# Routed third feed-forward: the second half's token rows scattered one per tile over sixteen tiles instead of two per tile over eight

## Chip, cores, metric

One core of one Trainium2 chip runs the whole program. The metric is device time in microseconds (us) of one execution. "Faster" or "slower" below is always against the kernel before.

## What is computed

Four layers, each an attention-like block and a feed-forward block, over x of 4 batches x 512 tokens x 128 features, f32. The change touches the third feed-forward, a mixture of 8 experts of which each token takes two:

```python
logits = jnp.einsum('bsd,de->bse', x, Wg)
top_vals, top_idx = jax.lax.top_k(logits, 2)
weights = softmax(top_vals) put at top_idx
for e in range(8):
    u, v = x @ W1[e], x @ W2[e]            # 128 -> 256 each
    out += ((u * sigmoid(u) * v) @ W3[e]) * weights[..., e][..., None]
```

## The kernel before, in words

Each engine has its own instruction stream; they meet at semaphores. The kernel doesn't run all experts over all tokens. It sorts the (token, choice) rows by expert into tiles of 128 rows, so that each tile belongs to one expert, and runs one small matrix chain per tile. The 4 batches are done in two halves (batches 0 and 1, batches 2 and 3). A half has HT = 8 token tiles and K1 = 2 choices, so 16 scatters of 128 rows each, and TILES2 = 23 expert tiles; NTILE2 = 46 tiles run in one unrolled loop over c. Tiles 0 to 22 are the first half, 23 to 45 the second.

What each engine does around the change:

- POOL (GpSimd). `scatter_in(half, i)` (L812) is an indirect DMA that writes 128 rows of 129 numbers (a token row and its row number) from SBUF into the table `tiles_in` in HBM, to the places that the routing found; each adds 16 to the semaphore `scattered`. `scatter_out(c)` (L831) waits for tile c's result (`y2_ready`) and writes its 128 rows with an indirect DMA into the table `tiles_out`. POOL runs its stream strictly in order. The first half's 16 scatters in are done before the loop. In the loop (L836 to L840) POOL does `scatter_out(c)`, and behind it, for c = 3 to 10, two of the second half's scatters in. I call the second half's scatters in by number, in 0 to in 15, and the scatters out by tile, out 0 to out 45.
- SP (SyncE) issues the loads of `tiles_in` in pairs of tiles (L690). Tiles sit in groups: 0-7, 8-15, 16-22, 23-30, 31-38, 39-45. The loads of group n wait until all scatters out of group n-2 have landed (L688). Before the first load of the second half (tile 23) SP also waits until all 16 of the second half's scatters in have landed (L706). Behind the loads of group 4 (tiles 31 to 38) it issues the loads of the first half's results (L700), which wait for out 22.
- PE (TensorE), in iteration c: `turn_in2(c+1)` (L1661) transposes the next tile and waits for its load; `up2(c)`; `turn_hidden2(c-1)` (L1684); `down2(c-2)`; then `beside_tiles(c)`. One of these calls is `load_word(1, w)` at c = 10, 13, 16: PE reads a word of SBUF into a register that says which experts the second half's tiles belong to. It is first used at c = 23 and waits for DVE's step `tiles2_1` (L3060).
- DVE (VectorE), in iteration c: `product2(c)` (L3126), `copy_hidden2(c-1)` (L3133), `copy_y2(c-2)` (L3141), which writes the result y of tile c-2. `copy_y2` of group 2 and later waits until the scatters out of group n-2 have landed, since the buffer is reused. At c = 28, 29 `combine2` (L3152, L3157) weighs the first half's two choices.
- ACT (ScalarE), in iteration c: `copy_in2(c+1)` and `gate2(c)`, both L1884, both waiting for PE.

So y of tile c comes in iteration c+2, behind the transposition of tile c+3, and everything on PE behind a transposition that waits for its load waits too. L853 is the helper for all other matmuls.

Of the kernel before, what the change touches and what calls it, by code (L numbers as in the profile page):

```python
# [35 lines left out]
E1, F1, K1 = 16, 176, 2  # L36
# [10 lines left out]
HT = 2 * TT  # L47
# [53 lines left out]
def build(nc, a, out):  # L101

    with ExitStack() as ctx:
# [6 lines left out]
        def sem(name):  # L110
            if name not in held:
                held[name] = ctx.enter_context(nc.semaphore(name))
            return held[name]
# [132 lines left out]
        def rows_of_choice(b, k):  # L246

            return token_rows[K1 * b + k]
# [484 lines left out]
        def _(pool):  # L733
# [72 lines left out]
            def scatter_in(half, i):  # L806

                t, k = divmod(i, K1)
                b = HALVES[half][t // TT]
                pool.wait_ge(setup, SETUP.index(f"places2_{half}") + 1)  # L810
                pool.wait_ge(sem("h_rows_ready"), NB + b + 1)
                nc.gpsimd.indirect_dma_start(  # L812
                    out=tiles_in, out_offset=bass.IndirectOffsetOnAxis(ap=routes2[half].scatter_at[:, k * HT + t:k * HT + t + 1], axis=0),
                    in_=rows_of_choice(b, k)[:, t % TT, :], in_offset=None, bounds_check=NTILE2 * P - 1,
                    oob_is_err=False).then_inc(sem("scattered"), 16)
# [11 lines left out]
            def scatter_out(c):  # L827
                group, slot = y2_place(c)
                pool.wait_ge(*tile_loaded(c))
                pool.wait_ge(sem("y2_ready"), c + 1)  # L830
                nc.gpsimd.indirect_dma_start(  # L831
                    out=tiles_out, out_offset=bass.IndirectOffsetOnAxis(ap=x2_in[:, slot, D:D + 1].bitcast(U32), axis=0),
                    in_=y2_rows[:, slot, :], in_offset=None, bounds_check=K1 * NTOK - 1,
                    oob_is_err=False).then_inc(y_stored[group % 2], 16)

            for c in range(NTILE2):  # L836
                scatter_out(c)
                if 3 <= c < 3 + HT:
                    for k in range(K1):
                        scatter_in(1, K1 * (c - 3) + k)  # L840

            for b in range(NB):
                pool.wait_ge(sem("rows3_ready"), b + 1)
# [4 lines left out]
        def _(pe):  # L848
# [752 lines left out]
            def count2(half, at):  # L1601

                chosen = routes2[half].chosen
                pe.wait_ge(setup, SETUP.index(f"chosen2_{half}") + 1)
                mm(psum[:, at, 0:HT * E2], before[:], chosen, True, False, skip_group_check=True)
                for t in range(1, HT + 1):
                    m = mm(psum[:, at, t * E2:(HT + 1) * E2], ones_b[:], chosen[:, 0:(HT + 1 - t) * E2], False, t == HT, skip_group_check=True)
                m.then_inc(sem("counted1"), 1)
# [17 lines left out]
            def load_word(half, w):  # L1626
                if w == 0:
                    pe.wait_ge(setup, SETUP.index(f"tiles2_{half}") + 1)
                words[half, w] = nc.tensor.value_load(routes2[half].tile_words[0:1, w:w + 1], min_val=0, max_val=8 ** 8 - 1)
# [77 lines left out]
            def turn_back2(b, at):  # L1707

                pe.wait_ge(sem("combined"), NB + b + 1)
                for t in range(TT):  # L1710
                    m = nc.tensor.transpose(psum[:, at, t * P:(t + 1) * P], gathered2[:, b % 2 * TT + t, 0, :], eye[:])
                m.then_inc(sem("batch_out"), 1)

            def center3(b, at):
                pe.wait_ge(x_ready, x_after(FFN2, b))
                mm(bank(at), center[:], x[:, b, :]).then_inc(sem("ln_centered"), 1)

            def variance3(b, at):
                pe.wait_ge(sem("ln_squared"), norm_of(ATTN3, b))
                pe.wait_ge(sem("ln_copied"), b + 1)  # L1720
                mm(bank(at), mean[:], squares3[b % 2]).then_inc(sem("ln_var"), 1)

            def project3(b, at):
                pe.wait_ge(ln_done, norm_of(ATTN3, b))
                mm(bank(at), w_3[:, W_IN, :], h[:, b, :]).then_inc(sem("proj3_done"), 1)

            def gate_x3(b, at):
                pe.wait_ge(sem("xw_ready"), b + 1)
                mm(bank(at), w_3[:, W_GX, :], xw[b % 2]).then_inc(sem("proj3_done"), 1)

            def gate_a3(b, at):

                if at >= 6:
                    pe.wait_ge(sem("gx_ready"), b + 1)
                mm(bank(at), w_3[:, W_GA, :], xw[b % 2]).then_inc(sem("proj3_done"), 1)
# [41 lines left out]
            def beside_tiles(c):  # L1777
                n = c - TILES2
                if c == 1:
                    pe.wait_ge(setup, SETUP.index("scores2_1") + 1)  # L1780
                    pe.wait_ge(sem("h_rows_ready"), NB + 3)
                    count2(1, 7)
                if c in (10, 13, 16):
                    load_word(1, (c - 10) // 3)
                for b in range(2):
                    at = 6 + b
                    if n == 6 + b:
                        turn_back2(b, at)
                    if n == 8 + b:
                        center3(b, at)  # L1790
                    if n == 10 + b:
                        variance3(b, at)
                    if n == 14 + b:
                        project3(b, at)
                    if n == 16 + b:
                        gate_x3(b, at)
                    if n == 18 + b:
                        gate_a3(b, at)

            turn_in2(0)  # L1800
            for c in range(NTILE2 + 2):
                if c + 1 < NTILE2:
                    turn_in2(c + 1)
                if c < NTILE2:
                    blocks[c] = block_of(c)
                    up2(c)
                if 1 <= c < NTILE2 + 1:
                    turn_hidden2(c - 1)
                if c >= 2:
                    down2(c - 2)  # L1810
                beside_tiles(c)
# [67 lines left out]
        def _(act):  # L1879
# [199 lines left out]
            def shared_gates(b):  # L2079
                act.wait_ge(sem("shared_up"), 2 * b + 2)  # L2080
                if b >= 1:

                    act.wait_ge(sem("shared_hid"), b)
                lo, _, hi = ((0, 4, 5), (2, 3, 1))[b % 2]
                f(shared_act0, bank(lo), ACT.Silu).then_inc(sem("shared_gate"), 1)
                f(shared_act1[HI:HI + F1R], psum[0:F1R, hi, :], ACT.Silu).then_inc(sem("shared_gate"), 1)
# [305 lines left out]
        def _(dve):  # L2392
# [408 lines left out]
            for _, hi in shared_hid:  # L2801
                v.memset(hi, 0.0)
# [4 lines left out]
            def shared_products(b):  # L2807
                _, up, hi = ((0, 4, 5), (2, 3, 1))[b % 2]
                for n, (src, gates_, dst, rr) in enumerate(((up, shared_act0, shared_hid[b % 2][0], slice(0, P)),
                                                            (hi, shared_act1, shared_hid[b % 2][1], slice(HI, HI + F1R)))):  # L2810

                    dve.wait_ge(sem("shared_gate"), 2 * b + n + 1)
                    dve.wait_ge(sem("shared_up"), 2 * b + 2)
                    if b >= 2:
                        dve.wait_ge(sem("shared_out"), b - 1)
                    m = v.tensor_tensor(dst[rr], psum[rr, src, :], gates_[rr], ALU.mult)
                m.then_inc(sem("shared_hid"), 1)
# [467 lines left out]
```

## Time and profile before

| | |
|---|---|
| median of 3 runs | 1105.28 us (1103.7 to 1110.93) |
| the profiled execution | 1108.78 us, its span 1107.0 us |
| busy share of the span | PE 84%, DVE 54%, ACT 45%, POOL 27% |
| tile loop of the third feed-forward | first matmul at about 885 us, last scatter out at 1016.79 us |
| granted TensorE clock over the span | 0.92 of full |

Times in the rows are us from the span's start. A timeline row is: start, duration, engine, line, operation, output<-input, count, and in brackets how long the engine had been idle and what ended that. Rows with a count merge neighbours. "issue" is a wait that nothing in the profile explains, "remote" one that ended with a semaphore event which the profile can't give to an engine of this core. PE's ends are modelled, not measured.

### The profile page before, as it was taken

The numbers are of one execution on the slowest core, as the hardware profiler recorded it, in microseconds if no ns is written. First come the engines' busy times: TensorE is split into PE (matmuls) and PEld (weight loads), VectorE is DVE, ScalarE is ACT, GpSimd is POOL, SyncE is SP. The second block draws the span as 40 slices with busy tenths as digits, with TensorE's granted clock in tenths as the row PEclk, the third lists the DMA queues.
The fourth block names the chain that finished last, engine by engine and source line by source line (L and its number), as shares of the span: only waits on it lengthen the run. The fifth ranks groups of instructions, "written<-read, shape, count | busy, mean of one in ns | idle before, by whom it ended". The sixth has DMA issues, their size and how long they took to land.

```text
span 1107.0 us, 12051 instructions
## 1 busy us (share of the span) xinstructions
PE 931.5 (84%) x3714; PEld 425.8 (38%) x3714; DVE 601.3 (54%) x1207; ACT 499.6 (45%) x937; POOL 300.9 (27%) x303
## 2 busy tenths in 40 slices
PE   5799999999799999998767984957877776887788
PEld 2344545454222222332233761422332344554433
DVE  2223233433888878777224445379998542545355
ACT  4233223233267667777632331665755421445720
POOL 9100000000001110110363561056756645433010
PEclk9799999999899999999969996988988886988889
DMA  8660000040011211210232206000000201311023
GB/s 175 183 235 0 1 1 1 1 93 0 23 52 49 77 49 51 59 43 3 55 105 70 56 26 189 8 11 1 0 1 7 69 28 53 100 33 50 3 77 114
DMA packets 81329, 59.52 MB, mean 54 GB/s; under 512 B 23422, under 2 KB 75704, under 8 KB 81172
## 3 DMA queue, kind: packets, MB, share of 16 engines
q1 hardware_dynamic: 74932, 51.00, 16.8%
q0 software_dynamic: 6336, 7.77, 2.3%
q8 instruction: 31, 0.51, 0.2%
q14 instruction: 30, 0.25, 0.1%
HBM read 38.41 MB, written 21.87 MB: 54 GB/s over the span
## 4 chain that ended last, share of the span: by engine, by line
PE 62%; DVE 12%; issue 11%; ACT 7%; another core or an unknown queue 2%; POOL 2%; SPq 2%; DMA 2%; DVEq 0%; POOLq 0%; ACTq 0%
PE psum L853 59%; ACT sb_scr L1884 3%; DVE sb_scr L2604 3%; DVE sb_scr L2979 2%; DVE sb_scr L2988 2%; POOL sb_scr L800 1%; ACT sb_qstack L1884 1%; ACT psum L1884 1%; SPq L629 1%; PE psum L1684 1%; PE psum L1009 1%; PE psum L1661 1%; SPq L634 0%; DVE sb_scr L2466 0%
## 5 line engine op out<-in xcount | busy, mean ns | idle before, releaser
L1884 ACT ACTIVATE sb_scr<-psum 128x512 f32<-128x512 f32 (+5 forms) x592 | 298.6, 539 | 367.1 <-PE psum L853 243.2
L2604 DVE TENSOR_REDUCE sb_scr<-psum 128x2 f32<-128x1024 f32 x128 | 154.7, 1222 | 40.3 <-PE psum L853 40.0
L761 POOL DMA_DIRECT2D sb_heads<-sb_scr x48 | 24.8, 523 | 439.6 <-DVE sb_scr L2620 439.3
L853 PE MATMUL psum<-sb_wide,sb_scr 128*128 (+1 forms) x532 | 120.8, 356 | 7.0 <-DVE sb_scr L3141 5.5
L800 POOL TENSOR_TENSOR sb_scr<-sb_scr 128x512 f32<-128x512 f32 x64 | 82.7, 1298 | 99.0 <-ACT sb_scr L1884 53.1
L853 PE MATMUL psum<-sb_kstack,sb_qstack 96*128 96x512 bf16 x256 | 98.2, 395 | 8.2 <-DVE sb_scr L2604 8.1
L853 PE MATMUL psum<-sb_qstack,sb_kstack 128*128 128x512 bf16 x256 | 99.0, 393 | 4.2 <-ACT sb_scr L1884 2.8
L2530 DVE TENSOR_SCALAR sb_scr<-psum,sb_b 128x512 f32<-128x512 f32 x48 | 34.6, 748 | 116.4 <-PE psum L853 116.4
L1884 ACT ACTIVATE sb_scr<-psum,sb_b 128x512 f32<-128x512 f32 x48 | 31.3, 685 | 142.9 <-PE psum L853 142.9
L853 PE MATMUL psum<-sb_h,sb_wide 128*128 128x512 f32 x192 | 88.3, 596 | 0.8 <-ACT sb_scr L1884 0.8
L853 PEld LDWEIGHTS psum<-sb_wide,sb_scr 128*128 128x128 f32 x532 | 76.4, 202 | 30.4 <-issue 28.5
L2979 DVE TENSOR_TENSOR_SCAN sb_scr<-psum,sb_scr 128x512 f32<-128x512 f32 x64 | 77.9, 1217 | 13.8 <-ACT psum L1884 13.7
L853 PE MATMUL psum<-sb_scr,sb_v 128*32 128x512 f32 x512 | 70.8, 625 | 4.8 <-ACT sb_scr L1884 4.2
L853 PE MATMUL psum<-sb_wparts,sb_pick 96*128 96x512 bf16 x128 | 43.0, 419 | 36.8 <-DVE sb_scr L2988 36.1
L853 PE MATMUL psum<-sb_scr,sb_eye 128*128 128x512 f32 x128 | 73.3, 658 | 0.8 <-DVE sb_scr L2988 0.5
L831 POOL DMA_INDIRECT tiles_out<-sb_scr x46 | 44.9, 976 | 74.2 <-DVE sb_scr L3141 62.5
L853 PEld LDWEIGHTS psum<-sb_qstack,sb_kstack 128*128 128x128 bf16 x256 | 24.9, 98 | 97.3 <-ACT sb_scr L1884 75.3
L853 PE MATMUL psum<-sb_scr,sb_wide 128*128 128x512 f32 x128 | 60.4, 594 | 0.0
L3126 DVE TENSOR_TENSOR sb_scr<-psum,sb_scr 128x256 f32<-128x256 f32 x46 | 19.5, 425 | 56.1 <-ACT sb_scr L1884 47.6
L789 POOL DMA_INDIRECT expert_out<-sb_scr,sb_row_at x40 | 38.9, 972 | 37.2 <-DVE sb_row_at L2839 15.0
L853 PEld LDWEIGHTS psum<-sb_h,sb_wide 128*128 128x128 f32 x192 | 34.5, 193 | 33.0 <-issue 31.9
L853 PE MATMUL psum<-sb_x,sb_center 128*128 128x512 f32 x64 | 37.8, 685 | 7.9 <-DVE sb_x L2624 5.2
(338 smaller groups left out, 1367.0 us busy)
## 6 DMA issues: line engine op xcount, KB each, us to landing
sb_qstack<-q_bounce SPq DMA_DIRECT2D x48, 96.0 KB
sb_kstack<-k_bounce SPq DMA_DIRECT2D x144, 32.0 KB
sb_scr<-pick_rows SPq DMA_DIRECT2D x8, 512.0 KB
sb_scr<-tiles_in SPq DMA_DIRECT2D x22, 129.0 KB
expert_in<-sb_scr SPq DMA_DIRECT2D x4, 645.0 KB, 6.1
tiles_in<-sb_scr SPq DMA_DIRECT2D x4, 645.0 KB, 8.3
sb_scr<-expert_in SPq DMA_DIRECT2D x8, 322.5 KB, 3.5
expert_out<-sb_scr SPq DMA_DIRECT2D x4, 512.0 KB, 4.9
```

Of the source, the lines that this page charges most:

```text
L629: sp.dma_start(weights1[q][0][:, :, at:at + hi - lo], a[f"L1_ffn_w_{n}"][2 * q:2 * q + 2, :, lo:hi].rearrange("e d f -> d e f")).then_inc( ...
L761: pool.dma_start(heads[at:at + DH, b % 2, :], head_out(n)[32 * j:32 * j + DH, :]).then_inc(sem(f"heads_packed{b % 2}"), 16)
L789: nc.gpsimd.indirect_dma_start(out=expert_out, out_offset=bass.IndirectOffsetOnAxis(ap=row_at[:, q % RX, j:j + 1], axis=0), in_=y_rows[:, ...
L800: nc.gpsimd.tensor_tensor(drive[:, n % RB, :], dtx[:, b, :], bcast_b[:, n % RB, :], ALU.mult).then_inc(sem("drive_ready"), 1)
L831: nc.gpsimd.indirect_dma_start(out=tiles_out, out_offset=bass.IndirectOffsetOnAxis(ap=x2_in[:, slot, D:D + 1].bitcast(U32), axis=0), in_=y ...
L853: return nc.tensor.matmul(out_, w, r, start=start, stop=stop, **kw)
L1884: return nc.scalar.activation(out_, in_, func, **kw)
L2530: v.tensor_scalar(hidden[:, c % 2, t, :], bank(t), b1[:, t, c:c + 1], 0.0, ALU.add, ALU.max).then_inc(sem("hid_dve"), 1)
L2604: v.reduce_max(headmax[:, g % 2, t:t + 2, j], banks, AX.X).then_inc(sem("maxed"), 1)
L2979: v.tensor_tensor_scan(state[:, i % RB, :], bank(4 + i % RD), drive[:, i % RB, :], 0.0, ALU.mult, ALU.add).then_inc(sem("scanned"), 1)
L2988: v.tensor_tensor(read[:, i % 2, :], bank(2 + i % RC), state[:, i % RB, :], ALU.mult).then_inc(sem("read_ready"), 1)
L3126: v.tensor_tensor(hid2[:, c % 2, :], psum[:, UP2_BANKS[c % 3], H2:2 * H2], gact2[:, c % 2, :], ALU.mult).then_inc(sem("hid2_ready"), 1)
```

## The change

POOL: behind each scatter out of tiles 3 to 18 there is one scatter in instead of two behind each of tiles 3 to 10. PE: the three `load_word(1, w)` are at c = 5, 6, 7 instead of 10, 13, 16. Nothing else differs.

```diff
             for c in range(NTILE2):
                 scatter_out(c)
-                if 3 <= c < 3 + HT:
-                    for k in range(K1):
-                        scatter_in(1, K1 * (c - 3) + k)
+                if 3 <= c < 3 + K1 * HT:
+                    scatter_in(1, c - 3)
@@ PE, beside_tiles(c)
-                if c in (10, 13, 16):
-                    load_word(1, (c - 10) // 3)
+                if c in (5, 6, 7):
+                    load_word(1, c - 5)
```

## Rows read from the trace of the kernel before

**Rows 1.** The page: the chain that ended last, its shares by engine

```profile
PE 62%; DVE 12%; issue 11%; ACT 7%; another core or an unknown queue 2%; POOL 2%; SPq 2%; DMA 2%; DVEq 0%; POOLq 0%; ACTq 0%
```

**Rows 2.** POOL's timeline in the loop; L831 scatters out, L812 scatters in

```profile
899.00 0.97 POOL L831 DMA_INDIRECT tiles_out<-sb_scr  x1 [0.46 <-issue]
900.28 0.97 POOL L812 DMA_INDIRECT tiles_in<-sb_scr,sb_v  x1 [0.30 <-issue]
...
913.05 0.97 POOL L812 DMA_INDIRECT tiles_in<-sb_scr,sb_v  x1 [0.30 <-issue]
917.21 0.98 POOL L831 DMA_INDIRECT tiles_out<-sb_scr  x1 [3.18 <-DVE sb_scr L3141]
...
931.26 0.97 POOL L812 DMA_INDIRECT tiles_in<-sb_scr,sb_v  x1 [0.30 <-issue]
935.36 0.97 POOL L831 DMA_INDIRECT tiles_out<-sb_scr  x1 [3.13 <-DVE sb_scr L3141]
...
944.47 0.97 POOL L831 DMA_INDIRECT tiles_out<-sb_scr  x1 [0.84 <-DVE sb_scr L3141]
...
949.74 0.97 POOL L831 DMA_INDIRECT tiles_out<-sb_scr  x1 [0.82 <-issue]
```

**Rows 3.** Busy time, clock and DMA by stretch: start:end length, PE, PEld, DVE, ACT, POOL

```profile
899.00:935.40 36.40, 20.68 (x76) 11.58 (x75) 9.18 (x28) 5.32 (x17) 23.38 (x25) 0.73 0.18 54
935.40:952.00 16.60, 16.60 (x78) 10.94 (x77) 7.87 (x25) 5.54 (x17) 8.34 (x9) 0.87 0.21 60
```

**Rows 4.** Timelines of PE, DVE and ACT around the second stall

```profile
924.70 0.69 PE L853 MATMUL psum<-sb_wide,sb_scr 128*128 x4
925.58 0.30 PE L1661 MATMUL psum<-sb_eye,sb_scr 128*128 128x128 f32 x1 [0.19 <-issue]
```
```profile
924.13 0.28 DVE L3141 COPY sb_scr<-psum 128x128 f32<-128x128 f32 x1
934.23 0.29 DVE L3141 COPY sb_scr<-psum 128x128 f32<-128x128 f32 x1 [3.78 <-remote]
```
```profile
916.11 0.55 ACT L1884 ACTIVATE sb_scr<-psum 128x128 f32<-128x128 f32 x2 [5.28 <-remote]
934.26 0.55 ACT L1884 ACTIVATE sb_scr<-psum 128x128 f32<-128x128 f32 x2 [6.68 <-remote]
```

**Rows 5.** POOL's timeline in the second feed-forward: first and last of 40 scatters out

```profile
609.93 0.99 POOL L789 DMA_INDIRECT expert_out<-sb_scr,sb_row_at  x1 [12.79 <-DVE sb_row_at L2839]
...
672.23 0.97 POOL L789 DMA_INDIRECT expert_out<-sb_scr,sb_row_at  x1 [0.30 <-issue]
```

**Rows 6.** SP's timeline: loads of tiles for groups 2 and 3, then first results

```profile
920.88 1.90 SPq L690 DMA_DIRECT2D sb_scr<-tiles_in  x4
946.77 1.58 SPq L690 DMA_DIRECT2D sb_scr<-tiles_in  x2
960.79 1.52 SPq L700 DMA_DIRECT2D sb_scr<-tiles_out  x3
```

**Rows 7.** PE's timeline: tile 23 turned, then the idle stretch ahead of tile 28

```profile
949.69 0.27 PE L1661 MATMUL psum<-sb_eye,sb_scr 128*128 128x128 f32 x1
951.45 0.27 PE L1661 MATMUL psum<-sb_eye,sb_scr 128*128 128x128 f32 x1
...
967.85 1.11 PE L1711 MATMUL psum<-sb_eye,sb_scr 128*128 128x128 f32 x4 [4.05 <-DVE sb_scr L3157]
968.76 0.42 PE L1661 MATMUL psum<-sb_eye,sb_scr 128*128 128x128 f32 x1
...
972.81 0.42 PE L1661 MATMUL psum<-sb_eye,sb_scr 128*128 128x128 f32 x1
...
975.76 0.27 PE L1661 MATMUL psum<-sb_eye,sb_scr 128*128 128x128 f32 x1
...
978.26 0.27 PE L1661 MATMUL psum<-sb_eye,sb_scr 128*128 128x128 f32 x1
```

**Rows 8.** DVE's timeline: the routing's last word, and y of tile 20

```profile
895.71 0.16 DVE L3060 TENSOR_SCALAR sb_v<-sb_v 1x3 uint32<-1x3 f32 x1
...
952.07 0.28 DVE L3141 COPY sb_scr<-psum 128x128 f32<-128x128 f32 x1
```

**Rows 9.** Busy time and granted clock by microsecond, behind PE's idle stretch

```profile
967.00:968.00 1.00, 0.15 (x1) 0.15 (x2) 1.00 (x5) 0.00 (x0) 0.00 (x0) 0.50 0.09 23
```

## The prediction

> **What bounds the kernel now.** I read the page first: the chain that ended last is mostly PE [rows 1], but shares over 1107 us say nothing about one stage, so I went to the stretch that the change touches, the tile loop from about 885 us. There I read POOL's timeline, since the change moves POOL's instructions, and then asked of each other engine what it waited for in the same stretch.
>
> POOL's timeline [rows 2] shows out 3 at 899.00 and out 11 at 935.36. Between them lie 24 instructions (8 scatters out, 16 in). Where POOL doesn't wait they start every 1.28 us (0.97 busy and 0.30 of issue). 24 x 1.28 is 30.7 us, and the stretch takes 36.4, that is 1.515 us for each slot. The missing 5.7 us are two waits for a y (3.18 and 3.13 us). So for eight tiles the loop goes at POOL's pace: 4.55 us a tile. Later, without scatters in, it goes at about 1.76 us a tile: out 15 at 944.47 and out 18 at 949.74 are 5.27 us apart for three tiles. The stretches agree [rows 3]: in the first PE is busy 20.7 of 36.4 us at a granted clock of 0.73 of full, in the next 16.6 of 16.6 us at 0.87.
>
> What is odd is that the other engines stall although they don't depend on POOL there. PE's down matmuls of tile 11 start at 924.70 and should be over by 925.4, but DVE copies that y at 934.23, waiting at the end on "remote", and ACT stands idle 6.68 us until 934.26 [rows 4]. POOL's last scatter of that run had started at 931.26 and was over by 932.2 [rows 2]. The first stall looks alike: POOL's run ends at 914.0, and ACT wakes at 916.11 after 5.28 us [rows 2, 4]. In both cases ACT and DVE come back 2 us after POOL falls silent, and POOL falls silent because it has caught up with them. I read this as an oscillation: an unbroken run of indirect DMAs holds up what waits for PE, until POOL runs dry. The second feed-forward has the same picture at another mix: 40 scatters, 39 slots from 609.93 to 672.23, so 1.60 us a slot [rows 5].
>
> The Trainium skill, page "SBUF — State Buffer", section "Who interferes with whom", says that a DMA never contends with a compute engine and that PE and ACT never wait on anyone. By that rule the stalls have another cause than POOL. It is the basis of one rival below.
>
> **The change, part by part.**
>
> POOL's order. No instruction is added or removed: 16 scatters in, 46 out. What changes is how far the scatters in reach. Before, in 15 comes right behind out 10, ahead of 935.36. After, it comes behind out 18. From out 3 to in 15 there are now 31 slots. Without a wait that is 31 x 1.28 = 39.6 us; at the pace of the loop before, 31 x 1.515 = 47.0 us; at that of the second feed-forward, 31 x 1.597 = 49.5 us [rows 2, 5]. I take 1.515, as it is the same loop and the same mix of buffers, and keep both others for the range. The tile chain needs only 1.76 us a tile and POOL, with two slots a tile, now 2.56, so POOL stays the slower of the two and its runs go on until the others stall. In 15 then starts at 899.0 + 47.0 = 946.0.
>
> What waits for it. SP may not load tile 23 before all 16 scatters in have landed, nor before out 15 has. Before, the second decided: out 15 at 944.47, the load issued at 946.77, 2.3 us later [rows 2, 6]. In a dense run landing takes longer: out 7 at 917.21, the next loads at 920.88, 3.7 us [rows 2, 6]. In 15 ends such a run, so I take 3.7. From the load's issue to the transposition of tile 23 it is at most 949.69 - 946.77 = 2.9 us, and PE wasn't idle there, so the load before had nearly no slack; from the transposition to y of tile 20 it is 952.07 - 949.69 = 2.4 us [rows 6, 7, 8]. After: 946.0 + 3.7 + 2.9 + 2.4 = 955.0 for y 20, against 952.07: 2.9 us late. The queue behind this wait: on SP the loads of groups 3 and 4 and the results of the first half; on PE `up2`, `turn_hidden2` and `down2` behind `turn_in2(23)`, and so y 20, 21 and 22, which come in the iterations behind.
>
> Nothing later takes it up. SP issues the first half's results at 960.79 only after out 22 and the loads of group 4, and PE stands idle 4.05 us for them before 967.85 [rows 6, 7]. That chain starts with y 22 and shifts as a whole.
>
> PE's clock. PE has done all it can by y 19, about 2 us after y 18, and then waits for tile 23: out 18 at 944.4, y 18 some 1.1 us ahead of it, the transposition at 952.6, so PE stands idle for about 6 us where it was busy before. After the idle 4.05 us the granted clock is 0.50, the 1.2 GHz level [rows 9], and the next tiles come 4.05 and 2.95 us apart (968.76, 972.81, 975.76) where the one after takes 2.50 [rows 7]: 2.0 us lost. I add 2.0. The page "TensorE: Matmul & The Clock Gate", section "HAM oscillation — how this bites in real kernels", of the Trainium skill tells of such waits for a DMA after which the engine starts cold; this trace agrees with its 0.50.
>
> The earlier part of the loop. Between 899 and 945 the tiles come more evenly, 3.0 us each, where they took 4.55 and then 1.8. That is no term of its own: it is in the 31 slots.
>
> The register loads. Three reads either way. Their word is ready at 895.87 [rows 8], PE comes to the read at c = 5 behind the down matmuls of tile 3, whose y goes out at 899.00 [rows 2], so a little ahead of that, and there is no new wait. One costs PE less than 0.9 us: that is all there is from the start of the down matmuls to the next transposition at c = 13, the matmuls included [rows 4]. At c = 5, 6, 7 POOL is already the slower one, as it was at c = 10 and 13. Zero; under 2.7 us if that cover is gone.
>
> Buffers. Group 2's loads wait for out 7, now at 899.0 + 8 x 1.515 = 911.1 instead of 917.21, so earlier. Zero.
>
> **Sum.** +2.9 + 2.0 = +4.9 us. Against the profiled execution's 1108.78 that is 1113.7; that execution lies 3.5 us above the median, so against 1105.28 it is 1110.2 us.
>
> **The rivals.**
>
> A. POOL's run goes on unbroken and nothing is lost (the other side: faster). The tile chain has more slack than before and may keep ahead of POOL in spite of the stalls. 31 x 1.278 = 39.6, in 15 at 938.6, y 20 at 947.6: -4.5 + 2.0 = -2.5 us, 1102.8. It decides once a slot costs under 1.36 us (31 x 1.357 = 42.1, where the sum is zero). For it: POOL has 15 tiles to draw on while 31 slots pass, 26.4 us of work for the chain in 39.6. Against it: POOL drew on three slots a tile before, which left the chain more room still (1.76 in 3.84 us), and ran dry twice all the same; and the second feed-forward's 1.60 us a slot shows that it was broken there too [rows 5].
>
> B. The stalls aren't POOL's, as the skill's page would have it. Then tiles 3 to 18 keep their times, out 18 is at 949.74, in 15 at 951.0, landed 2.3 later as in an easy stretch, y 20 at 951.0 + 2.3 + 2.9 + 2.4 = 958.6: +6.6 + 2.0 = +8.6 us, 1113.9. Against it: both stalls end 2 us behind POOL's last scatter [rows 2, 4].
>
> C. The oscillation gets shorter and costs more per slot: three tiles in a run (6 slots, 7.7 us) and then a wait of 3.1 us, 1.8 us a slot. In 15 at 954.8, y 20 11.7 us late, with the clock +13.7 us, 1119.0. It passes 1% at 1.71 us a slot. For it: a tile now carries POOL for two slots only, so the same number of tiles made before a stall gives a shorter run, and each run ends in the same wait. Against it: the waits may shrink with the runs.
>
> D. The change does nothing that counts: in 15 lands before tile 23 is wanted. That needs a slot of 1.28 us and a tile chain slower than before; I see no way but A.
>
> **How the numbers follow.** The sum 0.42, with slots of 1.45 to 1.65 us (1108 to 1115 us); A 0.22; B 0.16; C 0.15; 0.05 for anything else. A and the sum's lower part reach down to 1101, B lies at 1113.9, and the range goes to 1117, leaving out C's upper half and the unknown: 1101 to 1117. What a measurement of this kernel can tell from no change is about 1%, 11 us. Faster by more than that needs -11 us where even A gives -2.5: 0.04. Slower by more than that is C and the upper end of B: 0.16. Within: 0.80.
>
> **What would show it.** In the changed kernel: in 15's start less out 3's over 31, near 1.5 us (1.28 is A, 1.8 is C); tiles 3 to 10 as slow as before would be B. SP's load of tile 23 should come 2 to 4 us behind in 15 and no longer behind out 15, and PE should show an idle stretch of 3 to 7 us ahead of the transposition of tile 23, with a clock of 0.50 behind it. The idle 4 us ahead of tile 28 should be there unchanged. The prediction is wrong if ACT and DVE no longer show waits on "remote" in this loop at all, or if a stage outside it moves.

## The result, and the profile after

The changed kernel takes 1110.91 us (median of 15 runs, 1103.94 to 1115.42) where the kernel before takes 1105.57 (15 runs on the same chip, 1103.17 to 1111.76). The ratio is 1.0044, with a 95% interval of 1.0027 to 1.0061: 4.9 us slower, 3.0 to 6.7. That is within the 1% which the prediction called no change, but it isn't zero. Its profiled execution took 1109.63 us (span 1107.8) at a granted clock of 0.923. That is only 0.85 us more than the profiled execution of the kernel before, because its out 3 came 3.13 us earlier, ahead of the first instruction that was moved on POOL; the two traces are therefore compared from there on.

In the profile after, all lines of the kernel from L841 on have a number lower by one. First POOL's timeline in the loop, the answer to [rows 2]. The columns are start, duration, engine, line, operation, and in brackets the idle time before it and what ended that.

```profile
895.87 0.97 POOL L831 DMA_INDIRECT tiles_out<-sb_scr  x1 [0.52 <-issue]
897.14 0.97 POOL L812 DMA_INDIRECT tiles_in<-sb_scr,sb_v  x1 [0.30 <-issue]
...
905.49 0.97 POOL L831 DMA_INDIRECT tiles_out<-sb_scr  x1 [2.18 <-DVE sb_scr L3140]
...
918.03 0.97 POOL L831 DMA_INDIRECT tiles_out<-sb_scr  x1 [2.63 <-DVE sb_scr L3140]
...
933.28 0.97 POOL L831 DMA_INDIRECT tiles_out<-sb_scr  x1 [5.21 <-issue]
...
944.77 0.97 POOL L812 DMA_INDIRECT tiles_in<-sb_scr,sb_v  x1 [0.30 <-issue]
947.91 0.97 POOL L831 DMA_INDIRECT tiles_out<-sb_scr  x1 [2.17 <-issue]
954.27 0.97 POOL L831 DMA_INDIRECT tiles_out<-sb_scr  x1 [5.39 <-DVE sb_scr L3140]
```

Out 3 starts at 895.87 and in 15 at 944.77: 48.90 us for 31 slots, 1.577 us each. Inside a run (a row of instructions that POOL issues without waiting) they still start 1.28 us apart. Three waits break the runs (ahead of out 6, out 10 and out 14), where two broke them before.

Then PE's timeline where tile 23 comes in, the answer to [rows 7].

```profile
949.36 0.47 PE L1660 MATMUL psum<-sb_eye,sb_scr 128*128 128x128 f32 x1 [8.46 <-DMA sb_scr<-tiles_in]
...
969.38 0.66 PE L1710 MATMUL psum<-sb_eye,sb_scr 128*128 128x128 f32 x4 [3.78 <-DVE sb_scr L3156]
```

Before, PE wasn't idle ahead of the transposition of tile 23. Now it stands for 8.46 us and is released by the load. SP had issued that load at 947.15, 2.38 us behind in 15:

```profile
947.15 15.29 SPq L690 DMA_DIRECT2D sb_scr<-tiles_in  x8
962.54 2.07 SPq L700 DMA_DIRECT2D sb_scr<-tiles_out  x4
```

The result of tile 20, which used to come at 952.07 [rows 8], is now written at 953.15. By distance, y 20 comes 57.28 us behind out 3, where it came 53.07 behind it. The rows of DVE's timeline are y 19 to y 22:

```profile
946.79 0.29 DVE L3140 COPY sb_scr<-psum 128x128 f32<-128x128 f32 x1 [1.71 <-remote]
953.15 0.29 DVE L3140 COPY sb_scr<-psum 128x128 f32<-128x128 f32 x1
955.68 0.28 DVE L3140 COPY sb_scr<-psum 128x128 f32<-128x128 f32 x1
957.31 0.28 DVE L3140 COPY sb_scr<-psum 128x128 f32<-128x128 f32 x1
```

Last, busy time and granted clock by stretch (start:end, length, then PE, PEld, DVE, ACT and POOL, then the clock), which answers to [rows 3] and [rows 9].

```profile
895.90:935.40 39.50, 30.61 (x122) 18.72 (x121) 13.86 (x41) 8.50 (x27) 23.15 (x24) 0.83 0.16 48
...
945.00:950.00 5.00, 0.64 (x2) 0.43 (x3) 0.37 (x2) 0.13 (x1) 1.71 (x2) 0.50 0.43 116
...
952.00:953.00 1.00, 1.00 (x7) 1.00 (x6) 0.72 (x2) 0.25 (x1) 0.00 (x0) 0.50 0.00 0
953.00:954.00 1.00, 1.00 (x4) 0.49 (x3) 0.33 (x2) 0.28 (x1) 0.00 (x0) 0.53 0.00 0
954.00:955.00 1.00, 1.00 (x8) 0.71 (x7) 0.00 (x0) 0.41 (x2) 0.73 (x1) 1.00 0.00 0
...
968.00:969.00 1.00, 0.00 (x0) 0.00 (x0) 0.96 (x5) 0.00 (x0) 0.00 (x0) 1.00 0.29 88
969.00:970.00 1.00, 0.62 (x6) 0.62 (x6) 1.00 (x5) 0.00 (x0) 0.00 (x0) 1.00 0.07 11
```

The early part of the loop did become smoother: PE is busy 30.6 of 39.5 us, where it was busy 20.7 of 36.4. None of that reaches the end, because behind it PE waits for tile 23 and then works at half clock until about 954.

### The profile page after: what moved, and what is told of

Same layout as the page of the kernel before. It is cut to its first block and busy times, and to the rows that moved or that the text cites. A ratio compares the mean times of both kernels' runs of the same rounds, so it can differ in the third digit from the quotient of the medians.

```text
span 1107.8 us, 12051 instructions
## 1 busy us (share of the span) xinstructions
PE 930.5 (84%) x3714; PEld 426.4 (38%) x3714; DVE 600.9 (54%) x1207; ACT 499.3 (45%) x937; POOL 300.9 (27%) x303
## 5 line engine op out<-in xcount | busy, mean ns | idle before, releaser
L831 POOL DMA_INDIRECT tiles_out<-sb_scr x46 | 44.9, 975 | 78.5 <-DVE sb_scr L3140 59.4
L789 POOL DMA_INDIRECT expert_out<-sb_scr,sb_row_at x40 | 38.9, 973 | 36.1 <-DVE sb_row_at L2838 20.3
```

Source lines behind the costliest of these rows:

```text
L789: nc.gpsimd.indirect_dma_start(out=expert_out, out_offset=bass.IndirectOffsetOnAxis(ap=row_at[:, q % RX, j:j + 1], axis=0), in_=y_rows[:, ...
L831: nc.gpsimd.indirect_dma_start(out=tiles_out, out_offset=bass.IndirectOffsetOnAxis(ap=x2_in[:, slot, D:D + 1].bitcast(U32), axis=0), in_=y ...
```

## The experiments

The theory under test has two halves. Up to in 15 the loop goes at POOL's pace, so spreading the same instructions gains nothing; and the load of tile 23 has a deadline, so the spreading costs whatever in 15 is late. The rivals are that the register loads do it, that a smoother order has a worth of its own which the lateness hides, and that the stalls of ACT and DVE have nothing to do with POOL. Ratios are to the kernel before, run on the same chip and in the same series.

Times in the loop are compared as distances from out 0, because the stretch as a whole starts at different times in different executions. Out 0 to out 20 is 60.37 us before and 64.65 after. Each kernel has one trace, so how far such a distance varies from execution to execution isn't known; the ratios are of all timed runs.

**Lateness alone.** The kernel before, with its last scatter in moved from behind out 10 to behind out 18. One instruction moves; no other order changes.

```diff
-                        scatter_in(1, K1 * (c - 3) + k)
+                        if K1 * (c - 3) + k < K1 * HT - 1:
+                            scatter_in(1, K1 * (c - 3) + k)
+                if c == 18:
+                    scatter_in(1, K1 * HT - 1)
```

> The kernel before, with one instruction moved: the last scatter in (in 15) stands behind out 18 instead of behind out 10. This is the deadline of tile 23's load alone, without spreading. Theory: PE idles 5 to 7 us ahead of the transposition of tile 23 and comes back at a clock of 0.50; +6 to +9 us less the 1.3 us slot that the dense stretch loses, so 1110 to 1113 us, ratio 1.005 to 1.007. Rival (the load has slack that the profile hides, and the whole +5 us of the change comes from POOL's longer dense stretch): ratio 1.000.

Measured: ratio 1.0059 (1.0032 to 1.0086), 6.5 us slower. Out 0 to out 20 is 67.40 us, 7.0 more than before; but the profiled execution, 1121.70 us, is the slowest of the ten (median 1115.26). PE's timeline shows the same wait as in the changed kernel:

```profile
956.04 0.48 PE L1664 MATMUL psum<-sb_eye,sb_scr 128*128 128x128 f32 x1 [5.81 <-DMA sb_scr<-tiles_in]
```

So the deadline by itself costs about what the whole change costs (the intervals overlap). The difference between the two traces is that of their last scatters: in 15 starts 57.83 us behind out 0 here and 55.15 behind it in the changed kernel (2.7 us), and out 20 follows 9.57 and 9.50 us behind in 15.

**Spreading alone.** The changed kernel with its scatters in behind tiles 0 to 15 instead of 3 to 18: one a tile over sixteen tiles, but the last one three tiles earlier.

```diff
-                if 3 <= c < 3 + K1 * HT:
-                    scatter_in(1, c - 3)
+                if c < K1 * HT:
+                    scatter_in(1, c)
```

> The changed kernel with its 16 single scatters in moved three tiles ahead: behind tiles 0 to 15 instead of 3 to 18, so in 15 comes right behind out 15. Theory (POOL's pace of about 1.55 us a slot up to in 15, then the load of tile 23 behind in 15): the first three slots fill POOL's idle time ahead of 899, in 15 starts 31 to 32 slots behind out 0, near 941 us, the load of tile 23 no longer makes PE idle by more than 2 us, y 20 comes 3 to 5 us earlier than in the kernel before: 1100 to 1103 us, ratio 0.995 to 0.998. Rival (the stalls of ACT and DVE have nothing to do with POOL's order, only the late load of tile 23 costs): tiles keep their times, ratio 1.000.

Measured: ratio 0.9993 (0.9971 to 1.0016), no difference. Out 0 to out 20 is 60.18 us against 60.37. PE has no wait for a load of `tiles_in` left in this stretch, so the lateness is gone, and with it the loss. This kernel differs from the changed one in nothing but the place of the scatters in, so the loss went with their place; the early register loads are the same in both. I had expected 0.995 to 0.998 and missed: the waits moved. POOL's timeline behind in 15, the first row here, shows two gaps for a y of 3.06 and 2.23 us, although nothing but scatters out is left.

```profile
937.92 0.97 POOL L812 DMA_INDIRECT tiles_in<-sb_scr,sb_v  x1 [0.30 <-issue]
939.21 0.97 POOL L831 DMA_INDIRECT tiles_out<-sb_scr  x1 [0.31 <-issue]
943.24 0.97 POOL L831 DMA_INDIRECT tiles_out<-sb_scr  x1 [3.06 <-DVE sb_scr L3140]
945.11 0.97 POOL L831 DMA_INDIRECT tiles_out<-sb_scr  x1 [0.90 <-issue]
948.31 0.97 POOL L831 DMA_INDIRECT tiles_out<-sb_scr  x1 [2.23 <-DVE sb_scr L3140]
```

The granted clock from 940 to 955, 49 to 64 us behind out 0, is 0.77 here. In the kernel before it is 1.00 at the same distance (942.1 to 957.1). The start three tiles earlier is worth 6.8 us at y 15 (43.7 us behind out 0 against 50.5) and 0.2 at y 20 (59.1 against 59.3).

**Starting early alone.** The kernel before, with its pairs behind tiles 0 to 7.

```diff
-                if 3 <= c < 3 + HT:
+                if c < HT:
                     for k in range(K1):
-                        scatter_in(1, K1 * (c - 3) + k)
+                        scatter_in(1, K1 * c + k)
```

> The kernel before with its pairs of scatters in three tiles ahead: two behind each of tiles 0 to 7. Theory: three of the 24 slots fall into POOL's idle time ahead of out 3, the oscillation stays: 24 slots of 1.515 us from out 0 put out 8 at 36.4 us behind out 0, and from there 1.76 us a tile: out 20 at 57.5 us behind out 0 instead of 60.4; ratio 0.997 to 0.999. Rival (as one_from_0 showed, what the earlier start gains is lost again to the stall's tail and the slow clock): ratio 1.000.

Measured: ratio 1.0012 (0.9997 to 1.0028); out 0 to out 20 is 61.09 us. The 0.997 to 0.999 and 57.5 us that I expected were missed, and the rival named there, 1.000, came out. Together with the run above this bears on the second rival: with the last scatter in early enough, one a tile and two a tile can't be told apart (0.9993 and 1.0012, overlapping intervals). The traces leave 0.9 us for the smoother order; the timings alone don't exclude up to about 5.

**The register loads alone.** The kernel before, with the three reads at c = 5, 6, 7.

```diff
-                if c in (10, 13, 16):
-                    load_word(1, (c - 10) // 3)
+                if c in (5, 6, 7):
+                    load_word(1, c - 5)
```

> The kernel before with only the second part of the change: the three register loads on PE at c = 5, 6, 7 instead of 10, 13, 16. Theory: nothing, ratio 1.000 within 0.002. Rival (the reads of a register on PE at c = 10 and 13 stand near both stalls and take part in them): the stalls move or shrink, and the ratio leaves 1.000 by more than 0.003.

Measured: ratio 1.0019 (0.9990 to 1.0049), and 60.18 us from out 0 to out 20 against 60.37. The trace shows no cost; the timing includes zero, and doesn't exclude that the reads carry some of the 4.9 us.

**Are the stalls POOL's?** In this run the 16 scatters in are left out of POOL altogether. SP writes the same rows into the table with plain DMAs, in token order, so the second half isn't sorted by expert: the kernel leaves out the sort and doesn't compute the layer. It is there for its time alone.

```diff
@@ SP, ahead of the loads of group 2
+                    for i in range(K1 * HT):
+                        sp.dma_start(tiles_in[at:at + P, :], rows_of_choice(b, k)[:, t % TT, :])
@@ POOL
-                if 3 <= c < 3 + K1 * HT:
-                    scatter_in(1, c - 3)
```

> The changed kernel without POOL's 16 scatters in of the second half. SP writes the same 16 x 128 rows into the table with plain DMAs, one behind another and in the order of the tokens, so the rows are not sorted by expert; the rest runs as before. POOL is left with one scatter out a tile. Theory (an unbroken run of POOL's indirect DMAs stalls the others): no wait of ACT or DVE on remote in the tile loop, 1.8 us a tile from out 3 on, y 20 near 30 us behind out 3 instead of 53: 18 to 23 us faster, 1083 to 1088 us, ratio 0.980 to 0.984. Rival (the stalls aren't POOL's): they stay, ratio above 0.995.

Measured: ratio 0.9827 (0.9788 to 0.9866, four runs), some 19 us faster. Out 3 to out 18 takes 27.7 us, 1.85 a tile, and out 0 to out 20 39.07 us. No wait of ACT or DVE ends on "remote" any more. But POOL has also become free, so this run alone can't say whether it is the indirect DMAs or POOL's time.

**POOL busy, without the indirect DMAs.** The same, with two memsets on POOL in the place of each scatter in.

```diff
+                if 3 <= c < 3 + K1 * HT:
+                    fill(wconv)
+                    fill(conv_diag)
```

> As plain_writes (SP writes the second half's rows unsorted with plain DMAs; POOL has no scatter in), but in the place of each scatter in POOL does two memsets of 128x512, about 1.1 us with their waits. POOL is as busy as in the changed kernel, with half of the indirect DMAs. Theory (it is the density of POOL's indirect DMAs, not POOL being busy): POOL's pace of about 2.4 us a tile from out 3 to out 18 binds, but no wait of ACT or DVE on remote shows; out 18 near 36 to 39 us behind out 3, where the changed kernel needs 47.6; ratio 0.988 to 0.993. Rival (any unbroken POOL run stalls the others): remote waits stay, out 18 at 45 us or more, ratio above 0.996.

Measured: ratio 0.9887 (0.9857 to 0.9917, four runs). Out 3 to out 18 takes 36.1 us, 2.41 a tile, near the 2.56 of two indirect DMAs back to back, and again no wait ends on "remote". POOL is the slower one here (out 18 starts 9.4 us behind y 18). So it isn't that POOL is busy.

**The same DMAs, further apart.** Here all 62 indirect DMAs are back, and a memset stands behind each of those of tiles 3 to 18.

```diff
                 scatter_out(c)
                 if 3 <= c < 3 + K1 * HT:
+                    fill(wconv)
                     scatter_in(1, c - 3)
+                    fill(conv_diag)
```

> The changed kernel with a memset of 128x512 on POOL (about 0.5 us and its wait) behind every indirect DMA of tiles 3 to 18, out or in; nothing is left out. POOL's DMAs start 1.9 to 2.0 us apart instead of 1.28. Theory (an indirect DMA every 1.28 us is what stalls the others): no remote waits of ACT and DVE, POOL alone binds: in 15 starts 31 x 1.95 = 60 us behind out 3 instead of 48.9, so about +11 us to the changed kernel, 1118 to 1123 us. Rival (the stalls come with scatters into the table, at whatever pace): remote waits stay.

Measured: ratio 1.0086 (1.0048 to 1.0124, four runs), 1112.98 us, below the 1118 to 1123 that I expected. The slots are 1.68 us, not 1.95: the memset starts at the end of the DMA and takes the place of the 0.30 us of issue. No wait ends on "remote". But in 15 now comes 53.4 us behind out 3. Two rows of the list of waits (engine, line, what it waited for: us in total, times, longest):

```profile
ACT sb_scr L1891 <- PE psum L1668: 47.0, 24, 27.6
...
PE psum L1668 <- DMA sb_scr<-tiles_in: 29.9, 2, 26.9
```

The tile chain runs ahead without a stall and then PE waits 26.9 us at one stroke for tile 23. In this kernel no stall holds the loop: POOL's 31 slots do, at 1.68 us each, and they cost more than the stalls did.

**How far apart, and can it be had for less?** Three more, all with the scatters in behind tiles 0 to 15, so that in 15 isn't late, and with memsets of 256, 384 and 512 columns behind each indirect DMA (in the diff the first; the others have 0:3 and 0:4). They put the DMAs 1.46, 1.57 and 1.68 us apart, against 1.28 in the run without them.

```diff
                 if c < K1 * HT:
+                    fill(wconv[:, 0:2])
                     scatter_in(1, c)
+                    fill(conv_diag[:, 0:2])
```

> one_from_0 (one scatter in behind each of tiles 0 to 15) with a memset of 128x256 on POOL behind every indirect DMA of these tiles; nothing is left out. The indirect DMAs then start about 1.45 us apart instead of 1.28. Theory (the stall comes from indirect DMAs 1.28 us apart, and in spaced it was gone at 1.68): if 1.45 is wide enough, no remote waits, in 15 starts 31 x 1.45 = 45 us behind out 0 instead of 47.2, PE keeps its clock, y 20 about 4 to 8 us earlier than in the kernel before: ratio 0.993 to 0.997. If 1.45 is still too dense: remote waits stay, ratio 1.000 to 1.003. Rival (only runs of POOL beyond a length count, not the spacing): remote waits stay at this and the longer spacings.

> As gap_short with memsets of 128x384: indirect DMAs about 1.56 us apart. Theory: no remote waits or few, in 15 at 31 x 1.56 = 48.4 us behind out 0, ratio 0.996 to 1.000.

> As gap_short with memsets of 128x512: 1.68 us apart, the spacing at which spaced had no remote wait. Theory: no remote waits, in 15 at 31 x 1.68 = 52 us behind out 0, y 20 at about 60 us, ratio 1.000 to 1.002. Against spaced (1.0086) this is again the price of the three tiles by which in 15 is late.

| apart, us | longest wait on "remote", us | PE's waits for loads, us in all | out 0 to out 20, us | ratio |
|---|---|---|---|---|
| 1.28 | 4.0 | none | 60.18 | 0.9993 (0.9971 to 1.0016) |
| 1.46 | 3.1 | 7.2 | 58.74 | 1.0004 (0.9980 to 1.0027) |
| 1.57 | none | 18.6 | 60.37 | 1.0015 (0.9996 to 1.0034) |
| 1.68 | none | 22.8 | 63.67 | 1.0043 (1.0017 to 1.0069) |

The first run kept its stalls, and its ratio lies in the range expected for that case. The other two missed (0.996 to 1.000 and 1.000 to 1.002 expected): in 15 came 50.9 and 54.2 us behind out 0 instead of 48.4 and 52, of which 1.6 and 1.5 us are one pause (last section). The stalls go between 1.46 and 1.57 us. The rival that only the length of POOL's runs counts fell with that: at 1.57 and 1.68 the 24 instructions ahead of that pause are one unbroken run, where the longest before was 12. The memsets are in all three, and at 1.46 the stalls are there, so a memset in between isn't enough. What the stalls took comes back as waits for the loads, as PE's timeline of the run with 1.57 us shows for tiles 16 and 23:

```profile
920.16 0.48 PE L1668 MATMUL psum<-sb_eye,sb_scr 128*128 128x128 f32 x1 [5.44 <-DMA sb_scr<-tiles_in]
...
948.36 0.48 PE L1668 MATMUL psum<-sb_eye,sb_scr 128*128 128x128 f32 x1 [13.12 <-DMA sb_scr<-tiles_in]
```

The load's deadline shows in all of these at once: in the six kernels where PE waits for tile 23 (the changed one, the single late scatter in, the four with memsets), out 20 starts 9.4 to 9.6 us behind in 15. In the one without memsets from tile 0 it is 13.0, and there in 15 decides nothing.

I found no version with all of the work in it that is faster than the kernel before.

## Why the prediction was right, point by point

**What bounds the loop** held. The runs of POOL's instructions set the pace: a tile needs two slots instead of three, but in 15 is behind 31 slots, and it comes no earlier for it. Spreading alone gives 0.9993; taking the 16 instructions off POOL gives 0.9827.

**The pace of the 31 slots** was undersized: 1.577 us measured against 1.515, that is 48.90 us against 47.0, +1.9. This is the term of the sum that was too small. The upper bound from the second feed-forward, 1.597 [rows 5], would have been nearer. One place has 2.4 us, more than the whole difference: out 14 could have started 1.1 us behind y 14 (929.72), as out 20 does behind y 20, at 930.8, and started at 933.28 (its row names no releaser, [5.21 <-issue]). Without that the slot would be 1.50. What holds POOL there is open (last section). The picture of rival C, more and shorter runs with a wait behind each, was right in kind: three waits instead of two, of 2.2, 2.6 and 5.2 us. Its 1.8 us a slot was too much, as the first two waits shrank with the runs.

**Rival A** (POOL unbroken, 1.28 us a slot) fell: the slot is 1.577. Rival D, a change without effect on tile 23, fell with PE's 8.46 us.

**Rival B** (the stalls aren't POOL's, tiles 3 to 10 keep their times) fell twice. In the changed kernel out 3 to out 11 takes 24.7 us (895.87 to 920.58), where it took 36.4 [rows 2]. And the stalls vanish when the scatters in are taken away or set 1.57 us apart. The Trainium skill, page "SBUF — State Buffer", section "Who interferes with whom", says that DMA never contends with a compute engine and that PE and ACT never wait on anyone. Its rule is about ports, and no run here shows a port held; but read as in the prediction, that a dense row of DMAs can't hold up ACT and DVE, it doesn't agree with 4.0 us at 1.28 us apart and none at 1.57.

**From in 15 to y 20** the three terms were 3.7, 2.9 and 2.4 us. Measured: in 15 to the load 2.38 (-1.3), load to transposition 2.21 (-0.7), transposition to y 20 3.79 (+1.4). Taking 3.7 from a dense run was the mistake in the first: 2.3, the gap at out 15 of before, was the right one. The third is longer at the slow clock.

**The clock** was +2.0 and came out at 2.1. It is the 1.4 us above, and y 20 to y 22 in 4.16 us where they were 3.49 apart before, 0.7. The granted clock was 1.00 up to 943, fell to 0.50, the 1.2 GHz level, inside the idle stretch of 8.46 us (0.85 in microsecond 943, 0.50 from 944) and was back at 1.00 in microsecond 954. The prediction had an idle stretch of about 6 us, which is a slip: its own numbers, y 19 at 945.3 and the transposition at 952.6, give 7.3. In the trace PE had ended its work at 940.9, since y 18 came 3.8 us ahead of out 18 and not 1.1; DVE wrote y 19 only at 946.79, in another wait on "remote".

**The sum at y 20 and y 22.** At y 20: 57.28 - 53.07 = +4.2 us, and at y 22 +4.9, where the prediction had 2.9 and then 4.9 with the clock. The errors of the terms cancel: +1.9 - 1.3 - 0.7 = -0.1 us. The mechanism was right, but that the sum fits this well is luck.

**The idle stretch ahead of tile 28** was taken to shift as a whole, and it shifts, but not with what follows. It is 3.78 us instead of 4.05 [rows 7], and the granted clock stays at 1.00 in the microseconds 968 and 969, where it fell to 0.50 before [rows 9]. From PE's restart to out 45 it takes 47.97 us (969.38 to 1017.35), where it took 48.94 (967.85 to 1016.79). That gives back 1.0 us in this execution, which the sum didn't have: out 3 to out 45 is 121.48 against 117.79, +3.7, while the timed runs say +4.9 (3.0 to 6.7). Whether other executions keep the clock there isn't known.

**The register loads and the buffers** at zero: the trace of the register loads alone shows -0.2 us; its timing includes zero, from -1.1 to +5.4 us. Single scatters in from tile 0, which have the same early reads, end at 1.8 us above the kernel before at most. Group 2's loads went out at 910.57, earlier than 920.88 [rows 6], as predicted.

## What to carry to other kernels

A producer that is spread out has to be priced by its last instance against the consumer's deadline: here one scatter moved from behind out 10 to behind out 18 cost about as much as the whole change. Spreading the instructions of an engine over more iterations didn't help where that engine sets the pace; only taking them off it did (19 us for 16 of them, the stalls that went with them included). And where a stall is removed, look at what is next in line: at 1.57 us apart the stalls were gone, and PE waited 18.6 us for loads instead.

## What the runs showed of the hardware

**Dense indirect DMAs hold up those who wait for PE.** In the kernel before ACT idles up to 6.7 us [rows 4] for a result that PE has long produced. In the second feed-forward DVE idles 12.1 us once, while POOL issues 16 scatters in a row (544.79 to 565.2), and comes back 2.3 us behind the last of them:

```profile
567.48 0.75 DVE L2624 SCALAR_TENSOR_TENSOR sb_x<-psum,sb_bout,sb_x 128x512 f32<-128x512 f32 x1 [12.11 <-remote]
```

In the runs of the loop, at 1.28 us apart the waits are up to 4.0 us in the run with one a tile from tile 0, at 1.46 up to 3.1, at 1.57 and 1.68 there are none. Which part of the chip delays the wake-up stays open. It isn't density alone: eleven scatters at 1.28 us apart, from 864.65 to 878.43 in the kernel before, bring no wait on "remote".

**A pause at one certain indirect DMA.** In ten of the twelve kernels (the ten runs above, the changed kernel and the kernel before) POOL pauses at the 26th indirect DMA of the loop, whichever that is. These are the rows of two kernels, first out 9 of the run with pairs from tile 0, then in 12 of the one with 1.68 us spacing:

```profile
929.16 0.97 POOL L831 DMA_INDIRECT tiles_out<-sb_scr  x1 [5.57 <-issue]
```
```profile
934.36 0.97 POOL L812 DMA_INDIRECT tiles_in<-sb_scr,sb_v  x1 [1.69 <-issue]
```

The first of them waits for its y too; beyond that the pause is 2.7 us. Likewise 2.4 us are left of the 5.21 at out 14 in the changed kernel. The 26th is in 14 with 2.16 us in the one with early register loads, and out 14 with 1.61 us in the one with spaced tiles 3 to 18, and in 12 with 1.58 to 1.90 us in the four with one a tile from tile 0; the profile gives three of these to a copy of a y, but a scatter in doesn't wait for one in this kernel's code. In the two kernels without scatters in, the 26th is out 25, which starts 3.3 us behind its y where its neighbours ahead of it take 1.1 or 1.2, as this row of the first of them shows (y 25 was written at 939.89).

```profile
943.17 0.97 POOL L841 DMA_INDIRECT tiles_out<-sb_scr  x1 [2.83 <-DVE sb_scr L3148]
```

In the kernel before and in the one with a single late scatter in, the 26th has its ordinary 0.30 us. Memsets between the DMAs don't shift it. What holds POOL there is open.
